# Three-pass output product in the first stage, expert numbers loaded ahead of the waits, and closings by halves in a four-layer kernel

## The chip, the cores and the metric

The kernel runs on 1 core of a Trainium2 chip. The metric is the device time in microseconds, from one launch of the whole program; the time before is the median of 3 runs.

## The reference, cut to what matters

Input x has 32 batches of 64 channels by 1024 columns, 2048 rows in all. Four layers follow each other, each as `x = x + ffn(cond(x))`:

```
L0: cond: 64x64 channel matrix per batch, mixed from 8 by a small softmax net
    ffn:  logits = y route_w^T (8 experts), top 1; h = y A^T (8 x 16 columns);
          out = (gate * h) Bw      -> 2048x128 by 128x1024, the low-rank output product
L1: cond: grouped convolution, 9 taps, plus context; ffn: int8-like quantised 1024x1024 product
L2: cond: grouped convolution; ffn: base 1024x1024 product + bias
          + top 2 of 16 experts: delta = sum_j w_j (y A^T) B_e^T, A^T 1024x64, B_e 64x1024
L3: cond: mixed channel matrix; ffn: relu(y up)^2 down (1024 -> 2048 -> 1024),
          + latent product scaled by the sum of the top 2 gates; then layer norm, gamma, beta
out = x + ...
```

## The kernel before, in words

The rows are cut into 16 tiles of 128 x 1024. Five engines run one instruction list each, written out by hand, and meet through counting semaphores; nothing is planned at run time but loops and the expert numbers. Some TensorE products have f32 operands; most large products are made in three passes of rounded operands (`split_product`, L1992: high by high, high by low, low by high), with the high part a rounded copy and the low part the difference.

**First stage** (`phase_first`, L211). One loop over steps s. In a step TensorE makes: the convolution of tile s-5 in two halves (`conv`, L370) with the channel mixing of tile s between them (L443), a head product (`head`, L345) and transposes of a tile some steps ahead, the output product of tile s-1 (L462: two f32 products of 512 columns, `whT` by `wb`), and the transpose of the gated rows of tile s (L467). ScalarE copies the head (`head_out`, L480), shifts the windows of the convolution of the next step (`shift_windows`, L686, two copies), copies transposed tiles and then `whT` (L540). VectorE adds the context to the convolution's halves (`conv_out`, L575), makes the routing (L629 to L644), the column peaks (L651) and the sum x1 (L662). SP stores x1 (L276), waits until the store has landed, and then loads the convolution's windows of that tile from DRAM in eight transfers (`load_windows`, L679). Ahead of the loop VectorE rounds the weight of layer 1 (`weight_round`, L570), and SP loads weights, among them the taps of both convolutions; the second convolution's taps are read from 242 us on, in the next stage.

**Expert stage** (`phase_l2`, L1276). Pairs of row and expert are sorted into 47 tiles of one expert each (groups of four). For each tile TensorE waits for the part of the operand and for the copies of the tile before last out of its two banks (L1925), loads the expert's number from SBUF into a register (`value_load`, L1926), and makes four passes (L1929). ScalarE and VectorE copy half the result each (L1562, L1769) into one of four buffers, and POOL scatters it to DRAM by an indirect DMA (L1511); a buffer is written again when its DMA has landed. Products of the base weight stand between the groups.

**Last stage** (`phase_l3`, L2000). Tokens are done in two halves of 8 tiles. At the end of each half `downward_both` (L2342) makes a tile's two column halves, 12 passes each, in two banks, and tells VectorE once, behind both. VectorE sums the halves (`add`, L2223), makes the mean (L2282), finishes the tile before (`finish`, L2249: reciprocal of the root, scaling and sum with x, L2256) and centres this one (L2246); ScalarE makes the sum of squares and the root (L2155, L2158); POOL stores each tile (L2123) and waits for the stores at the very end. Behind the first half TensorE's gate product (L2368) waits until all sums are made.

## Time and profile before

| | |
|---|---|
| median of 3 runs | 1641.01 us (1634.74 to 1644.5) |
| profiled execution, own time | 1638.99 us |
| its span | 1637.3 us |
| TensorE products busy | 1571.9 us, 96% |
| VectorE, ScalarE, POOL busy | 822.8, 507.2, 313.1 us |
| mean granted TensorE clock | 0.992 |

The span is the time from the first to the last instruction. Busy times are shares of it; an engine that is not on the chain of waits may be idle at no cost. PE is TensorE's product, PEld its weight load, DVE VectorE, ACT ScalarE, POOL GpSimd, SP SyncE, and a q behind an engine's name (PEq, SPq) its sequencer or queue of DMA issues.

### The profile page before, as it was taken

What the parts mean: (1) busy time and instruction counts of PE and PEld (TensorE: products, weight loads), DVE (VectorE), ACT (ScalarE), POOL (GpSimd) and SP (SyncE); (2) the same over time, 40 slices, a digit from 0 to 9 for tenths busy, and PEclk for the clock granted to TensorE, in tenths of its full rate; (3) what the DMA queues carried; (4) which work ended last, traced back from release to release, by engine and by line L of the source; (5) the groups of instructions that cost most, each with busy time, mean ns of one, the idle gap of its engine ahead of it and who ended that gap; (6) DMA issues with size and microseconds to landing.
All of it is one profiled execution on the core that took longest, in us unless ns stands there. A gap on an engine that the chain in (4) does not pass through costs nothing.

```text
span 1637.3 us, 20655 instructions
## 1 busy us (share of the span) xinstructions
PE 1571.9 (96%) x7752; PEld 1281.6 (78%) x7752; DVE 822.8 (50%) x1336; ACT 507.2 (31%) x763; POOL 313.1 (19%) x262
## 2 busy tenths in 40 slices
PE   8899889999998889999999999999999999999996
PEld 6787668889875568877888888887788888888875
DVE  4767688885574548762333333333633333333336
ACT  4443434433284512223222222212242222222122
POOL 2000022334084520121210011112012100111110
PEclk9999999999999999999999999999999999999998
DMA  9866634556755758883621111115826211111115
GB/s 318 240 191 193 144 118 159 186 191 208 278 174 176 271 180 312 309 306 135 114 81 38 50 51 51 52 52 175 288 77 113 83 38 50 51 51 51 52 41 178
DMA packets 117241, 238.57 MB, mean 146 GB/s; under 512 B 22503, under 2 KB 61551, under 8 KB 115778
## 3 DMA queue, kind: packets, MB, share of 16 engines
q1 hardware_dynamic: 81034, 155.27, 28.8%
q0 software_dynamic: 23008, 68.24, 14.0%
q10 hardware_dynamic: 13120, 14.00, 3.0%
q8 instruction: 51, 0.84, 0.2%
q14 instruction: 28, 0.23, 0.0%
HBM read 164.51 MB, written 89.19 MB: 155 GB/s over the span
## 4 chain that ended last, share of the span: by engine, by line
PE 76%; DVE 5%; POOL 3%; issue 2%; DMA 2%; ACT 1%; SPq 0%; DVEq 0%; POOLq 0%; ACTq 0%
PE pu L1996 27%; PE pd L1996 26%; PE l_po L1996 7%; PE pf L1996 5%; POOL scratch_pairs L1504 2%; PE l_ea L1353 2%; PE pw L675 2%; PE pw L674 2%; PE l_ea L1929 1%; DMA scratch_expert_out<-expert_out,pair_ids 1%; PE l_po L1929 1%; PE l_ea L1944 1%; PE l_tr L1944 1%; DVE y1T L977 0%; PE pd L2368 0%
## 5 line engine op out<-in xcount | busy, mean ns | idle before, releaser
L1996 PE MATMUL pd<-down_hi,hid_hi 128*128 128x512 f32 x640 | 249.1, 389 | 2.9 <-issue 2.9
L1996 PE MATMUL pu<-y_hi,up_hi 128*128 128x512 f32 x640 | 250.7, 392 | 0.6 <-issue 0.6
L1996 PE MATMUL pu<-y_lo,up_hi 128*128 128x512 f32 x640 | 250.3, 391 | 0.0
L1996 PE MATMUL pu<-y_hi,up_lo 128*128 128x512 f32 x640 | 250.2, 391 | 0.0
L1996 PE MATMUL pd<-down_lo,hid_hi 128*128 128x512 f32 x640 | 249.0, 389 | 0.0
L1996 PE MATMUL pd<-down_hi,hid_lo 128*128 128x512 f32 x640 | 249.0, 389 | 0.0
L2297 DVE TENSOR_TENSOR hid_lo<-hidden,hid_hi 128x512 fp32r<-128x512 f32 x64 | 44.3, 693 | 391.5 <-ACT hid_hi L2205 391.5
L2127 POOL TENSOR_TENSOR down_lo<-raw,down_hi 128x1024 fp32r<-128x1024 f32 x40 | 100.5, 2511 | 681.0 <-ACT down_hi L2142 681.0
L2199 ACT ACTIVATE hidden<-pu 128x512 f32<-128x512 f32 x64 | 38.3, 598 | 470.0 <-PE pu L1996 470.0
L2236 DVE TENSOR_TENSOR acc<-pd,acc 128x512 f32<-128x512 f32 x224 | 143.6, 685 | 54.7 <-PE pd L1996 51.4
L1996 PEld LDWEIGHTS pd<-down_hi,hid_hi 128*128 128x128 f32 x640 | 120.1, 188 | 28.7 <-issue 3.7
L1996 PEld LDWEIGHTS pu<-y_hi,up_hi 128*128 128x128 f32 x640 | 121.0, 189 | 26.4 <-issue 1.1
L1996 PEld LDWEIGHTS pu<-y_hi,up_lo 128*128 128x128 f32 x640 | 120.9, 189 | 25.5
L1996 PEld LDWEIGHTS pu<-y_lo,up_hi 128*128 128x128 f32 x640 | 120.8, 189 | 25.0
L1996 PEld LDWEIGHTS pd<-down_lo,hid_hi 128*128 128x128 f32 x640 | 120.3, 188 | 24.9
L1996 PEld LDWEIGHTS pd<-down_hi,hid_lo 128*128 128x128 f32 x640 | 120.1, 188 | 24.8
L1996 PE MATMUL pf<-cbT,z_hi 128*128 128x512 f32 x240 | 97.6, 407 | 5.4 <-DVE z_lo L991 5.4
L1996 PE MATMUL l_po<-l_base_hi,l_y2s_hi 128*128 128x512 f32 x256 | 101.3, 396 | 0.0
L1996 PE MATMUL l_po<-l_base_hi,l_y2s_lo 128*128 128x512 f32 x256 | 99.8, 390 | 0.0
L1996 PE MATMUL l_po<-l_base_lo,l_y2s_hi 128*128 128x512 f32 x256 | 99.8, 390 | 0.0
L1996 PE MATMUL pf<-cbT,z_lo 128*128 128x512 f32 x240 | 94.6, 394 | 0.0
L688 ACT COPY Xs<-X 64x1016 f32<-64x1016 f32 x32 | 33.3, 1040 | 88.4 <-DMA X<-scratch_x 81.6
(329 smaller groups left out, 2495.3 us busy)
## 6 DMA issues: line engine op xcount, KB each, us to landing
l_x<-scratch_x SPq DMA_DIRECT2D x32, 512.0 KB, 6.5
delta<-scratch_expert_out SPq DMA_DIRECT2D x32, 512.0 KB, 7.0
raw<-in_up SPq DMA_DIRECT2D x32, 512.0 KB, 3.7
raw<-in_down SPq DMA_DIRECT2D x32, 512.0 KB, 4.4
X<-scratch_x SPq DMA_DIRECT2D x248, 64.0 KB, 2.6
y1T<-in_x SPq DMA_DIRECT2D x16, 512.0 KB, 8.6
scratch_x<-y1T SPq DMA_DIRECT2D x16, 512.0 KB, 3.3
scratch_x<-l_x SPq DMA_DIRECT2D x16, 512.0 KB, 5.6
```

Source lines behind the costliest of these rows:

```text
L674: pe.matmul(cols, x[:, b * GROUPS + g, :], taps[0][:, g, :], start=True, stop=False)
L675: last = pe.matmul(cols, xs[:, b * GROUPS + g, :], taps[1][:, g, :], start=False, stop=True)
L688: act.copy(xs[0:CH, :, 0:P - 1], x[0:CH, :, 1:P]).then_inc(sem, 1)
L1353: last = pe.matmul(ea[t % 2][:, 0:R2 + E2], prior["y2"][:, t % 2, k, :], war[:, k, :], start=k == 0, stop=k == KC - 1)
L1504: pool.indirect_dma_start(SC["pairs"], bass.IndirectOffsetOnAxis(ap=pos[:, n:n + 1], axis=0), val[:, n, :], None).then_inc(val_stored, 16)
L1929: last = pe.matmul(out_banks[i % 2][h][:], rT[g % 2][part][:, n * P:(n + 1) * P], B[:].rearrange("p e o -> p (e o)")[:, bass.ds(at + h * H ...
L1944: last = pe.matmul(py[t % 2][h][:, c * P:(c + 1) * P], x3[t][:, (4 * h + c) * P:(4 * h + c + 1) * P], mats[:, t % 2, :], start=True, stop= ...
L1996: mm = pe.matmul(out, lhs[a], rhs[b], start=first and n == 0, stop=last and n == len(pairs) - 1)
L2127: pool.tensor_tensor(dn[u][i][1][:], raw[i][:], dn[u][i][0][:].bitcast(F32), ALU.subtract).then_inc(dn_lo, 1)
L2199: act.activation(act_f[:, k % 2, :], pu[q], ACT.Relu).then_inc(relu, 1)
L2236: last = dve.tensor_tensor(part, bank, part, ALU.add)
L2297: dve.tensor_tensor(hid[u][1][:, i, cols], pu[q] if lat else act_f[:, k % 2, :], hid[u][0][:, i, cols].bitcast(F32), ALU.subtract).then_in ...
```

## The change

The low-rank output product of the first stage is made by `split_product` in three passes of rounded parts. The weight is split once ahead of the loop (high by ScalarE, low by VectorE); each step ScalarE rounds `whT` into `whT_hi` behind the copy, and VectorE makes `whT_lo`. The low part of the weight lies where the second convolution's taps lay until now, so these taps are loaded by SP behind the last windows of the stage; the first convolution waits for two taps transfers and no longer for four. The expert number is loaded ahead of the three waits. The closing products signal each column half by itself, VectorE sums them one by one (the last tile of each half: first half, finish of the tile before, second half), and the very last tile is scaled by halves and stored by SP and by ScalarE.

```diff
@@ -204,6 +204,8 @@
     names["h"], names["wh"], names["whT"] = at("h_mixed", 190656, [P, P + E0]), at("wh", 191200, [P, P]), at("whT", 191712, [P, P])
+    names["whT_hi"], names["whT_lo"] = [at("whT_" + part, 192320 + 512 * i, [P, P], F32R) for i, part in enumerate(("hi", "lo"))]
+    names["wb_hi"], names["wb_lo"] = at("l0_wb_hi", 210880, [P, D], F32R), at("l0_wb_lo", 153536, [P, D], F32R)
     names["small"] = at("l0_small", 192224, [P, 24])
...
@@ -286,6 +289,9 @@
                     load_windows(sp, SC["x1"], t, X[t % XS], X_loaded[t % XS], range(0, KC, 1 if t < NT - 2 else 2))
+            sp.wait_ge(o_mm, 2 * NT)
+            for i in range(2):
+                sp.dma_start(K["taps"][1][i][:], A["taps"][1, i]).then_inc(K["taps_loaded"], 16)
 
@@ -370,7 +376,7 @@
                     if t == 0:
-                        pe.wait_ge(K["taps_loaded"], 16 * 4)
+                        pe.wait_ge(K["taps_loaded"], 16 * 2)
                         pe.wait_ge(scb_out, 2)
@@ -452,14 +458,16 @@
                 if 0 <= s - 1 < NT:
-                    pe.wait_ge(whT_made, s)
+                    pe.wait_ge(w_lo, s)
                     if s == 1:
                         pe.wait_ge(agg_out, 8)
+                        pe.wait_ge(wb_split, 2)
                         pe.wait_ge(K["wb_loaded"], 16)
...
                             pe.wait_ge(x1_made, 2 * (s - 2) + i + 1)
-                        pe.matmul(po[i][:], whT[:], wb[:, i * HALF:(i + 1) * HALF], start=True, stop=True).then_inc(o_mm, 1)
+                        cols = slice(i * HALF, (i + 1) * HALF)
+                        split_product(pe, po[i][:], (whT_hi[:], whT_lo[:]), (wb_hi[:, cols], wb_lo[:, cols]), True, True).then_inc(o_mm, 1)
                 if s < NT:
@@ -515,6 +523,8 @@
                     turned_x(t + 2)
+            act.wait_ge(K["wb_loaded"], 16)
+            act.copy(wb_hi[:], wb[:]).then_inc(wb_split, 1)
             for s in range(NT + LAG0 - 1):
@@ -538,6 +548,10 @@
                     act.copy(whT[:], pm[:, 2 * P:3 * P]).then_inc(whT_made, 1)
+                    act.wait_ge(whT_made, s + 1)
+                    if s >= 1:
+                        act.wait_ge(w_lo, s)
+                    act.copy(whT_hi[:], whT[:]).then_inc(w_hi, 1)
                 t = {NT - 1: NT - 2, NT + 1: NT - 1}.get(s)
@@ -617,12 +631,17 @@
                 weight_round(c)
+            dve.wait_ge(wb_split, 1)
+            dve.tensor_tensor(wb_lo[:], wb[:], wb_hi[:].bitcast(F32), ALU.subtract).then_inc(wb_split, 1)
             dve.wait_ge(desc_made, E2)
...
                     conv_out(t, 0)
+                if 1 <= s <= NT:
+                    dve.wait_ge(w_hi, s)
+                    dve.tensor_tensor(whT_lo[:], whT[:], whT_hi[:].bitcast(F32), ALU.subtract).then_inc(w_lo, 1)
                 if s < NT:
@@ -792,6 +811,8 @@
     def conv_half(pe, t, b):
+        if t == 0 and b == 0:
+            pe.wait_ge(K["taps_loaded"], 16 * 4)
         if b == 0:
@@ -1918,12 +1939,12 @@
             g, n = i // 4, i % 4
+            at = pe.value_load(expert_of[0:1, i:i + 1], min_val=0, max_val=(E2 - 1) * D)
             if n == 0:
...
                 pe.wait_ge(eo_dve, i - 1)
-            at = pe.value_load(expert_of[0:1, i:i + 1], min_val=0, max_val=(E2 - 1) * D)
             for h in range(2):
...
@@ -2096,6 +2117,9 @@
                 pair(NPAIR * half + j, j, j % 2, True)
+        sp.wait_ge(last_made, 1)
+        sp.dma_start(tile_of(out, NT - 1)[:, 0:HALF], acc[:, HT - 1, 0:HALF]).then_inc(last_stored, 16)
+        sp.wait_ge(last_stored, 32)
 
@@ -2119,6 +2143,8 @@
                     T = HT * (half - 1) + t
+                    if T == NT - 1:
+                        continue
                     pool.wait_ge(out_made, T + 1)
@@ -2128,7 +2154,7 @@
         steps(body)(pool)
-        pool.wait_ge(out_stored, 16 * NT)
+        pool.wait_ge(out_stored, 16 * (NT - 1))
 
@@ -2212,6 +2238,8 @@
         steps(body)(act)
+        act.wait_ge(last_made, 2)
+        act.dma_start(tile_of(out, NT - 1)[:, HALF:D], acc[:, HT - 1, HALF:D]).then_inc(last_stored, 16)
 
@@ -2220,10 +2248,13 @@
 
-        def add(g, t, half, lat_back, first, end):
-            dve.wait_ge(dn_mm, HT * g + 2 * (t + 1) if end else HT * (g + 1) + t + 1)
+        def add(g, t, half, lat_back, first, end, halves=(0, 1)):
+            if not end:
+                dve.wait_ge(dn_mm, HT * (g + 1) + t + 1)
             T = HT * half + t
-            for h in range(2):
+            for h in halves:
+                if end:
+                    dve.wait_ge(dn_mm, HT * g + 2 * t + h + 1)
                 part, bank = acc[:, t, h * HALF:(h + 1) * HALF], pd[t % 2][h][:]
@@ -2253,8 +2284,14 @@
             dve.wait_ge(x3b_loaded[T % 2], 16 * (T // 2 + 1))
-            dve.scalar_tensor_tensor(out=acc[:, T % HT, :], in0=scratch[:], scalar=inv[:, T:T + 1], in1=x3b[:, T % 2, :],
-                                     op0=ALU.mult, op1=ALU.add).then_inc(out_made, 1)
+            if T < NT - 1:
+                dve.scalar_tensor_tensor(out=acc[:, T % HT, :], in0=scratch[:], scalar=inv[:, T:T + 1], in1=x3b[:, T % 2, :],
+                                         op0=ALU.mult, op1=ALU.add).then_inc(out_made, 1)
+                return
+            for h in range(2):
+                cols = slice(h * HALF, (h + 1) * HALF)
+                dve.scalar_tensor_tensor(out=acc[:, T % HT, cols], in0=scratch[:, cols], scalar=inv[:, T:T + 1],
+                                         in1=x3b[:, T % 2, cols], op0=ALU.mult, op1=ALU.add).then_inc(last_made, 1)
 
@@ -2274,9 +2311,12 @@
                     T = HT * (half - 1) + t
-                    if t == HT - 1:
+                    if t < HT - 1:
+                        add(g, t, half - 1, lat_back, first, end)
+                    else:
+                        add(g, t, half - 1, lat_back, first, end, (0,))
                         finish(T - 1)
-                    add(g, t, half - 1, lat_back, first, end)
+                        add(g, t, half - 1, lat_back, first, end, (1,))
 
@@ -2353,7 +2393,7 @@
                                          [w[:, h * HALF:(h + 1) * HALF] for w in dn[v][i]], n == 0, n == 3)
-            last.then_inc(dn_mm, 2)
+                last.then_inc(dn_mm, 1)
 
@@ -2449,7 +2489,7 @@
         K["kept_loads"] = [(K["l0_wa"][:], A["l0_wa"], K["wa_loaded"]), (K["l0_wb"][:], A["l0_wb"], K["wb_loaded"])]
-        K["kept_loads"] += [(K["taps"][c][i][:], A["taps"][c, i], K["taps_loaded"]) for c in range(2) for i in range(2)]
+        K["kept_loads"] += [(K["taps"][0][i][:], A["taps"][0, i], K["taps_loaded"]) for i in range(2)]
         K["kept_loads"] += [(K["gate"][:], A["gate"], K["l2_loaded"])]
```

Hunks left out only name buffers and semaphores. `split_product` (L1992), which is called now, makes for each pair (high, high), (high, low), (low, high) one matmul into the same bank.

## Rows read from the trace of the kernel before

**Rows 1.** The page; window 507-589 us: busy by engine, clock, DMA share, GB/s.

```profile
span 1637.3 us, 20655 instructions
PE 1571.9 (96%) x7752; PEld 1281.6 (78%) x7752; DVE 822.8 (50%) x1336; ACT 507.2 (31%) x763; POOL 313.1 (19%) x262
...
507.00:589.00 82.00, 63.97 (x255) 42.59 (x256) 41.61 (x72) 39.15 (x70) 43.75 (x45) 0.98 0.65 236
```

**Rows 2.** The page, part 4: the chain that ended last, by engine.

```profile
PE 76%; DVE 5%; POOL 3%; issue 2%; DMA 2%; ACT 1%; SPq 0%; DVEq 0%; POOLq 0%; ACTq 0%
```

**Rows 3.** Timeline of a step of the first stage: start us, us, engine, line, operation [idle before].

```profile
91.86 1.88 PE L462 MATMUL po<-l_wb,whT 128*128 128x512 f32 x4
92.55 1.04 ACT L689 COPY Xs<-X 64x1016 f32<-64x1016 f32 x1
93.58 0.27 PE L467 MATMUL pmix<-ident,wh 128*128 128x128 f32 x1
93.66 0.30 PEld L674 LDWEIGHTS pv<-taps,X 128*128 128x128 f32 x2 [0.36 <-issue]
```

**Rows 4.** The chain in order of time: start us, us, engine, line, passes.

```profile
588.88 10.92 PE l_po L1996 x48
```

**Rows 5.** Timeline of the first stage, steps 14 to 16.

```profile
144.75 0.69 DVE L580 TENSOR_TENSOR y1T<-pv,ctx 128x512 f32<-128x512 f32 x1
146.72 0.29 DVE L644 TENSOR_TENSOR wh<-h_mixed,l_small 128x128 f32<-128x128 f32 x1
150.38 0.69 DVE L580 TENSOR_TENSOR y1T<-pv,ctx 128x512 f32<-128x512 f32 x1
152.74 1.04 ACT L688 COPY Xs<-X 64x1016 f32<-64x1016 f32 x1 [3.88 <-DMA X<-scratch_x]
```

**Rows 6.** Timeline: VectorE at the start, and the two splits of 128x1024.

```profile
46.28 0.35 DVE L629 SCALAR_TENSOR_TENSOR h_mixed<-sumA,bias,pmix 128x136 f32<-128x136 f32 x1
...
1190.86 1.04 ACT L2137 CAST up_hi<-raw 128x1024 fp32r<-128x1024 f32 x1
1191.94 1.23 DVE L2219 TENSOR_TENSOR up_lo<-raw,up_hi 128x1024 fp32r<-128x1024 f32 x1 [0.26 <-ACT up_hi L2137]
```

**Rows 7.** Timeline of SP's queue in the first stage, TensorE behind it; the second convolution's taps (by tile).

```profile
87.84 0.43 SPq L276 DMA_DIRECT2D scratch_x<-y1T  x1
92.33 4.17 SPq L683 DMA_DIRECT2D X<-scratch_x  x8
...
103.34 0.46 PE L674 MATMUL pv<-taps,X 128*128 128x128 f32 x2 [1.05 <-issue]
...
L674 PEld LDWEIGHTS pw<-taps,X x256: 187/192/192, 242.4 to 428.4; 128*128 128x128 f32 x128
```

**Rows 8.** Number load (by line); timeline; waits (us, times, longest).

```profile
L1926 PEldq TENSOR_LOAD <-expert_of x47: 296/548/1207, 506.3 to 586.8; - x47
...
509.58 0.68 DVE L1769 COPY expert_out<-l_ea 128x512 f32<-128x512 f32 x1
511.16 0.49 PE L1929 MATMUL l_ea<-l_B,pair_rT_hi 128*128 x1 [1.81 <-DVE expert_out L1769]
...
PE l_ea L1929 <- DVE expert_out L1769: 10.5, 7, 2.6
```

**Rows 9.** The chain in order of time: a copy, and two landings of the indirect DMA.

```profile
537.17 0.70 DVE expert_out L1769
...
539.24 3.91 DMA scratch_expert_out<-expert_out,pair_ids
...
573.90 8.56 DMA scratch_expert_out<-expert_out,pair_ids
```

**Rows 10.** Timeline and chain of the two closings.

```profile
1176.00 0.40 PE pd L2368
...
1624.65 1.43 DVE acc L2232 x4
...
1629.73 0.53 POOL L2123 DMA_DIRECT2D out<-acc  x1 [4.18 <-DVE acc L2256]
```

More of the change, by code:

```diff
@@ L218, in phase_first @@
             buf[n] for n in ("pack rows agg bk h0 h1 lg ex att m z rz attT ctx12 bias3 scb den quo scb127 tmp xT hp h wh whT small").split()]
+        whT_hi, whT_lo, wb_hi, wb_lo = [buf[n] for n in ("whT_hi", "whT_lo", "wb_hi", "wb_lo")]
         kern, wa, wb, X, Xs = K["kern"], K["l0_wa"], K["l0_wb"], K["X"] + [buf["X"]], K["Xs"] + [buf["Xs"]]
@@ L245, in phase_first @@
         x1_stored, X_loaded = s_.slot_sems("x1_stored", 4), s_.slot_sems("X_loaded", XS)
-        (xT_mm, xT_made, h_mm, hp_made, m_mm, tabled, route, wh_made, wh_turned, whT_made, o_mm, x1_made, Xs_made, conv_done,
+        (xT_mm, xT_made, h_mm, hp_made, m_mm, tabled, wb_split, w_hi, w_lo, route, wh_made, wh_turned, whT_made, o_mm, x1_made, Xs_made, conv_done,
          y_made, topped, early_mm, early_out) = s_.sems(
-            "xT_mm xT_made h_mm hp_made m_mm tabled route_step wh_made wh_turned whT_made o_mm x1_made Xs_made conv_done "
+            "xT_mm xT_made h_mm hp_made m_mm tabled wb_split whT_hi_made whT_lo_made route_step wh_made wh_turned whT_made o_mm x1_made Xs_made conv_done "
             "y1_made y1_topped early_mm early_out")
@@ L2022, in phase_l3 @@
         "gate_mm gateT_made gate_turned gate_out gate_topped gate_summed")
-    gamma_loaded, eps_set, centred, ssq_made, rooted, inverted, weighed, out_made = s_.sems(
-        "gamma_loaded eps_set neg_mean_made sum_sq_made root_made rstd_made weighed out_made")
+    gamma_loaded, eps_set, centred, ssq_made, rooted, inverted, weighed, out_made, last_made, last_stored = s_.sems(
+        "gamma_loaded eps_set neg_mean_made sum_sq_made root_made rstd_made weighed out_made last_made last_stored")
     Q = 2 * NB
```

## The prediction

> **What bounds the kernel now.** I read the page, then the chain that ended last, then the waits and the timeline of the three places that the change touches. The page says that TensorE is busy for 1571.9 of 1637.3 us [rows 1], and the chain runs through its products for most of the span, with only 2% in issue and 3% on POOL [rows 2]. An edit can therefore win only where TensorE itself does less, or where it stands still and the edit touches what it waits for. Three such places are edited: the first stage (0 to 184 us, one tile of 128 rows per step), the expert stage (507 to 589 us, 47 tiles), and the two closings, at 1174 us and at the end. The profiled execution took 1639.0 us round its span of 1637.3; the median of the three runs is 1641.0, 2.0 above it, and the three lie between 1634.7 and 1644.5.
>
> **The product of the first stage.** Each step has one pair of f32 products, 512 columns each. A f32 product shows as two records; the four of a pair begin at 91.86 us, and 1.72 us later, at 93.58, follows the transpose [rows 3]: 0.43 us a record, 0.86 a product. A pass of rounded operands over 512 columns takes 10.92/48 = 0.2275 us [rows 4]. A pair in three passes is 6 x 0.2275 = 1.37 us: TensorE is relieved of 0.36 us a step, 5.7 us in 16 steps. That is the upper end of the gain, and I don't count on it, for what else ends the steps:
>
> In steps 5 to 12 (those with a head product, 8.4 us each) ScalarE copies the head out at 91.19 and then shifts the windows in two copies, the last from 92.55 to 93.59; the weights of the next convolution load at 93.66, after an idle of 0.36 us [rows 3]. TensorE has finished its own queue at the same moment (the transpose begins at 93.58 and holds it for 0.1). A shorter product only lengthens the wait for the shift: gain 0.03 us a step, which I call nothing.
>
> In steps 1 to 3 no windows are waited for and the products stand in line before the next transpose: 3 x 0.36 = 1.1 us gained. In step 4 VectorE ends the wait, so nothing. In steps 13 to 15 VectorE has no gap: its sum of one step begins at 144.75 and that of the next at 150.38, 5.63 us apart and neither behind an idle time [rows 5]. It gets the new subtraction, 128x128; the nearest row is the gated copy of that size at 0.29 us [rows 5]. The windows of the third step on are loaded by SP behind those sums, and ScalarE waits 3.88 us for them at 152.74 [rows 5]; so one such subtraction, +0.3 us, comes on the path, instead of a gain. From 155 us on TensorE runs without a stop to the end of the stage, with one pair in it: -0.36.
>
> The new waits: TensorE's pair waits for the low part, which is made behind VectorE's sum of the convolution (95.75 us) and so at about 96.8, while the next pair begins one period of 8.43 us behind 91.86, at 100.3 [rows 3]: 3 us of cover, under 1 us in steps 13 to 15. ScalarE makes the high part right behind the transposed copy, where nothing waits for it until the next head. On VectorE the routing of the tile is queued behind the subtraction and moves by 0.3 us; its result is wanted over 1 us later. These cost nothing; without cover a step would pay 0.3 + 0.3 us.
>
> The weight's own split is new at the start: a copy of 128x1024 on ScalarE (row of that form: 1.04 us) and a subtraction of 128x1024 on VectorE (1.23 us) [rows 6]. VectorE is the late one there: it rounds weights until 46.28 and starts the first routing at once [rows 6]. The copy fits beside the last rounding, the subtraction doesn't: +1.25 us before the first tile. Less the share of step 1 already won, the first x1 is stored about 0.9 us later. From there SP sets the pace: it stores x1, waits for the landing, then issues eight window loads of 4 us. The store of 87.84 is followed by its windows only at 92.33, when it has landed, and these windows let TensorE begin only at 103.34, after 1.05 us idle [rows 7]. So the 0.9 us arrive there whole, and the 1.1 won on TensorE don't help. The taps of the second convolution leave this queue and go behind the last windows; they are first read at 242.4 us, long after [rows 7]. They stood behind all the weight loads, so nothing comes sooner by it. First stage: +0.9 + 0.3 - 0.36 = +0.85 us. Bounds: -5.7 (every pass saved counts) and +3.7 (1.25 at the start and 0.6 of unhidden copies in four steps).
>
> **Expert numbers.** For each tile TensorE's sequencer waits for the copies of the tile before last, then loads the number (0.30 to 1.21 us, median 0.55), works on registers, and issues [rows 8]. Where the wait was long, the whole comes after it: the copy ends at 510.26 (509.58 + 0.68), and the product starts at 511.16. With the load ahead of the wait about 0.8 of these 0.9 us go. VectorE's copies ended 7 such idle times of 10.5 us in all [rows 8]. A group of four tiles has one long wait; with all 12 groups at 0.8 us the most that can come off is 9.6 us. Where the copies are there in time the load already starts as soon as the previous tile is issued, and the move changes nothing.
>
> What is late next? Each output tile goes: VectorE's copy, POOL's indirect DMA (0.95 + 0.30), its landing, and only then the copy of the tile four later into that buffer. In the trace a copy begins at 537.17, the DMA is issued at 539.24 and has landed at 543.15 [rows 9]: 6.0 us, and 6.3 until the next copy runs. A group of four tiles takes not much more (82 us by 12 is 6.8). So of two groups one is crossed by way of the store, which stays, and one by way of TensorE, where about 1 us goes: 0.5 us a group. Seven groups with such waits give 3.5 us; the first tiles about 0.5, the last ones, behind the long landing of 573.90, about 0.7. I take 0.7 off because the stores come closer together, with the DMA engines already 0.65 busy here [rows 1]. Estimate -4.0 us, between -9.6 and 0.
>
> The Trainium skill, "DMA: Bandwidth & Descriptors", section "Latency and other measured facts", gives a floor of about 600 ns for a tensor load. The trace has loads of 296 ns, so the measurement decides. By the page's figure each hidden load would give 0.6 us and no less, 47 of them 28 us if all stood on the path, which the loop above excludes.
>
> **Closings.** The last tile's two sums take 1.43 us together and begin at 1624.65, because VectorE is finishing the tile before [rows 10]. With a semaphore for each half, the first half of a tile is free 12 passes or 2.7 us sooner, and VectorE sums it in an idle time; that pulls the whole line of VectorE forward by 0.67. On the last tile the order becomes first half, finish of the previous tile, second half: 1622.7, 1623.45, then the second sum from 1624.86 to 1625.53, where it now ends at 1626.08. Gain 0.5. The same in the middle, where the gate's product waits for the sums until 1176.00: another 0.5 [rows 10]. Then the output by halves: POOL's issue runs now from 1629.73 to 1630.26 [rows 10]. Afterwards the second half goes out by ScalarE's queue, as soon as it is scaled; the gap ahead of POOL (0.3 us) and part of its 0.53 go, and the transfer is 256 KB beside 256 KB under way: -0.5. Closings: -1.5 us, bounds -2.5 and -0.5.
>
> The same page's section on one software DMA ("Anatomy of one DMA") gives 2.0 us fixed and the bytes at 436 GB/s: 3.2 us for 512 KB and 2.6 for 256. By that the last landing alone would give 0.6 us, in place of the 0.5 for the whole end of the store. No row here parts a landing into these two.
>
> **Sum.** +0.85 - 4.0 - 1.5 = -4.65 us: 1634.3 for an execution like the profiled one, and about 1636 beside the median of 1641.
>
> **Rivals.** (a) The stores don't bind: their landings stay near 4 us and the expert stage gives its 9.6, the first stage about 0, the closings 1.5. Then -11 us: 1630. For it: most copies in the stage don't wait for a landing. Against: the landing at 573.90 already takes 8.56 us [rows 9]. Chance 0.22. (b) The stores bind wholly, each us saved on TensorE is waited for again at a buffer: expert stage 0, sum -0.65, 1640. For it: landings stand on the chain at 539 and 573 us [rows 9]. Chance 0.20. (c) Slower: in the first stage the delay of the first x1 and the extra VectorE work per step are passed on through SP's chain, 1.25 us at the start and 0.3 us in each of eight or nine steps, +3.7 us, while the expert stage gives under 1 us and the closings 0.5. Sum about +2.5, 1643.5. It decides from the point at which the expert stage gives less than the first stage takes. Chance 0.10. The forecast keeps 0.48.
>
> A measurement of this kernel can't tell under about 0.5% (8 us) from no change. Forecast and (b) lie within it, (c) as well unless the runs scatter; (a) lies beyond. With the scatter of the medians, some 3 us, I give 0.27 to faster, 0.68 to the same, 0.05 to slower. Range: from (a), 1629, to (c), 1643.
>
> **What would show it.** In the trace after: pairs at about 1.37 us with the step still 8.4 us long and a longer idle before the convolution's weights; the first routing at about 47.5; the convolution now at 103.34 at about 104.2; the stage's last VectorE piece near 184.4 instead of 183.6. In the expert stage gaps behind copies of 0.2 to 0.3 us instead of 0.8 and more, and more waits of the copies for landings; the base products behind the stage start near 585.7 after correction for the first stage's shift, instead of 588.9. At the end the last sum ends 0.5 us nearer to the last product. I am wrong if the first stage is shorter by over 1 us (then SP was not its pace), or if the expert stage changes by under 1 or over 7 us.

## The result, and the profile after

The changed kernel takes 1626.80 us, the median of 12 runs (1622.94 to 1634.35), against 1639.34 us for 12 runs of the kernel before: a ratio of 0.9923, interval 0.9906 to 0.994, or 12.5 us faster. In a second series of 6 runs it was 1630.77 against 1639.97, 9.2 us faster. The forecast was 4.65 us and a range down to 1629. The time lay below the range: the direction was right, the size was not.

The profiled execution of the changed kernel happens to be the longest of its 12 (1634.35 us, span 1632.6). Its granted clock is 0.987 on the mean, where before it was 0.992, so whole stages of the two traces are not to be subtracted.

```profile
span 1632.6 us, 20788 instructions
PE 1575.3 (96%) x7784; PEld 1295.0 (79%) x7784; DVE 826.9 (51%) x1354; ACT 511.9 (31%) x780; POOL 310.6 (19%) x261
```

Busy TensorE is 1575.3 us against 1571.9 [rows 1], but at a lower granted clock. The kernel with the three-pass product alone (e1 below), profiled at the clock of the kernel before, 0.992, shows what the passes are worth:

```profile
PE 1567.9 (96%) x7784; PEld 1286.4 (79%) x7784; DVE 824.8 (50%) x1353; ACT 512.5 (31%) x780; POOL 310.9 (19%) x262
```

TensorE is busy for 4.0 us less there, and that kernel is no faster. The time did not come from less work.

**The end.** The first two fences are the transfers by issue (KB each, median us from issue to landing) before and after, the third is the timeline after.

```profile
out<-acc POOLq DMA_DIRECT2D x1, 512.0 KB, 2.9
```

```profile
out<-acc SPq DMA_DIRECT2D x1, 256.0 KB, 2.0
out<-acc ACTq DMA_DIRECT2D x1, 256.0 KB, 2.1
```

```profile
1627.51 1.41 DVE L2293 SCALAR_TENSOR_TENSOR acc<-scratch,l_rstd,l_x3b 128x512 f32<-128x512 f32 x2
1628.29 0.34 SPq L2121 DMA_DIRECT2D out<-acc  x1
1628.96 0.34 ACTq L2242 DMA_DIRECT2D out<-acc  x1
```

Before, the last issue began at 1629.73 [rows 10] and landed 2.9 us later, at 1632.6; the span ended at 1637.3, 4.7 us behind the landing. After, the second half was issued at 1628.96 and landed 2.1 us later, at 1631.1; the span ended at 1632.6, 1.5 us behind it. The timeline has no row for the stretch behind the landing, but the view of the kernel's last source line has: each engine's list is closed by an instruction called DRAIN. Its duration (ns: shortest, median, longest) and start, before and then after:

```profile
L2456 POOLq DRAIN  x1: 3164/3164/3164, 1632.8 to 1632.8; - x1
```

```profile
L2496 POOLq DRAIN  x1: 3082/3082/3082, 1628.2 to 1628.2; - x1
L2496 SPq DRAIN  x1: 7/7/7, 1631.2 to 1631.2; - x1
```

Before, POOL waited for the last landing, began its DRAIN 0.2 us behind it and ended it 3.16 us later, at 1636.0; the remaining 1.3 us are the closing of the program. After, POOL waits for the store before the last, so its DRAIN of 3.08 us runs beside the last store and is over at 1631.3; SP, which waits for the last landing, has a DRAIN of 7 ns at 1631.2. The same 1.3 us follow.

**The expert stage.** Waits (us in total, times, longest) of the copies for a landing, before and after, and the products that wait for a copy after.

```profile
ACT expert_out L1562 <- DMA scratch_expert_out<-expert_out,pair_ids: 10.5, 8, 4.9
DVE expert_out L1769 <- DMA scratch_expert_out<-expert_out,pair_ids: 5.7, 4, 4.3
```

```profile
ACT expert_out L1583 <- DMA scratch_expert_out<-expert_out,pair_ids: 23.6, 23, 3.2
DVE expert_out L1790 <- DMA scratch_expert_out<-expert_out,pair_ids: 14.9, 18, 1.7
PE l_ea L1950 <- DVE expert_out L1790: 6.4, 10, 1.4
```

The copies wait for landings 41 times (38.5 us in all), where it was 12 times (16.2 us). The timeline of a copy and the product behind it:

```profile
529.84 0.69 DVE L1790 COPY expert_out<-l_ea 128x512 f32<-128x512 f32 x1 [0.38 <-DMA scratch_expert_out<-expert_out,pair_ids]
530.82 0.50 PE L1950 MATMUL l_ea<-l_B,pair_rT_hi 128*128 x1 [0.48 <-DVE expert_out L1790]
```

The copy ends at 530.53 and the product starts at 530.82: 0.29 us, in place of 0.90 [rows 8].

**The first stage.** Timeline after, of the start, and of one pair of products in three passes:

```profile
45.95 1.23 DVE L635 TENSOR_TENSOR l_wb_lo<-l_wb,l_wb_hi 128x1024 fp32r<-128x1024 f32 x1
47.09 0.35 DVE L648 SCALAR_TENSOR_TENSOR h_mixed<-sumA,bias,pmix 128x136 f32<-128x136 f32 x1
48.81 0.33 PE L475 MATMUL pmix<-ident,wh 128*128 128x128 f32 x1 [1.20 <-DVE wh L663]
52.85 0.78 PE L2017 MATMUL po<-l_wb_hi,whT_hi 128*128 128x512 f32 x1
54.51 1.52 DVE L681 TENSOR_TENSOR y1T<-po,y1T 128x512 f32<-128x512 f32 x2 [2.36 <-PE po L2017]
...
93.52 0.48 PE L2017 MATMUL po<-l_wb_hi,whT_hi 128*128 128x512 f32 x1
...
95.00 0.27 PE L475 MATMUL pmix<-ident,wh 128*128 128x128 f32 x1
95.43 0.30 PEld L693 LDWEIGHTS pv<-taps,X 128*128 128x128 f32 x2 [0.51 <-issue]
95.46 0.46 PE L693 MATMUL pv<-taps,X 128*128 128x128 f32 x2 [0.18 <-issue]
...
101.98 0.48 PE L2017 MATMUL po<-l_wb_hi,whT_hi 128*128 128x512 f32 x1
```

VectorE's new subtraction puts the first routing at 47.09 instead of 46.28 [rows 6]; TensorE stands still for 1.20 us, and the first three-pass product then shows 0.78 us for a record where a later one shows 0.48: the granted clock had fallen. The windows view (us, busy by engine, granted clock, DMA share, GB/s) of 51 to 55 us and of the stretch behind the middle closing shows it, before and after:

```profile
51.00:55.00 4.00, 3.55 (x20) 2.19 (x18) 2.53 (x5) 1.62 (x4) 0.00 (x0) 1.00 0.07 25
1192.00:1200.00 8.00, 8.00 (x30) 6.42 (x29) 3.35 (x11) 2.57 (x4) 2.46 (x1) 0.79 0.41 131
```

```profile
51.00:55.00 4.00, 3.74 (x14) 3.37 (x15) 1.50 (x6) 1.77 (x4) 0.00 (x0) 0.57 0.00 0
1192.00:1200.00 8.00, 8.00 (x38) 6.71 (x38) 4.13 (x12) 4.21 (x6) 2.48 (x1) 1.00 0.39 126
```

0.57 over 51 to 55 us is nearly all at the lower level, 1.2 GHz. Later, at the full clock, a pair takes 1.48 us, from 93.52 to 95.00, where it was 1.72 [rows 3]. The idle time ahead of the next convolution's weights is longer instead, as foreseen: 0.51 us where it was 0.36 [rows 3]; and the next pair begins at 101.98, 8.46 us behind this one, where the step was 8.43 us long. A shorter product, the same step.

### The profile page after: what moved, and what is told of

Read it like the earlier page. It is cut to its first block, busy times and chain, and to the rows that moved or that the text cites. A ratio compares the mean times of both kernels' runs of the same rounds, so it can differ in the third digit from the quotient of the medians.

```text
span 1632.6 us, 20788 instructions
## 1 busy us (share of the span) xinstructions
PE 1575.3 (96%) x7784; PEld 1295.0 (79%) x7784; DVE 826.9 (51%) x1354; ACT 511.9 (31%) x780; POOL 310.6 (19%) x261
## 4 chain that ended last, share of the span: by engine, by line
PE 76%; DVE 5%; DMA 3%; POOL 2%; issue 2%; ACT 1%; SPq 0%; DVEq 0%; POOLq 0%; ACTq 0%
PE pu L2017 27%; PE pd L2017 26%; PE l_po L2017 7%; PE pf L2017 6%; POOL scratch_pairs L1525 2%; DMA scratch_expert_out<-expert_out,pair_ids 2%; PE l_ea L1374 2%; PE pw L694 2%; PE pw L693 2%; PE l_ea L1965 1%; PE l_tr L1965 1%; PE pg L1142 1%; DVE expert_out L1790 0%; DVE y1T L998 0%; PE pd L2408 0%
## 5 line engine op out<-in xcount | busy, mean ns | idle before, releaser
L2017 PEld LDWEIGHTS pf<-cbT,z_hi 128*128 128x128 f32 x240 | 47.5, 198 | 18.6 <-DVE z_lo L1012 8.8
```

Source lines behind the costliest of these rows:

```text
L2017: mm = pe.matmul(out, lhs[a], rhs[b], start=first and n == 0, stop=last and n == len(pairs) - 1)
```

## Marks that can be compared

In every profile I read the same places: the start of the first sum x1; the start of the last column maximum of the first stage; the first and last start of an expert product; the start of the last product; the end. A dip is a stretch at the lower level of the granted clock. Most dips cost TensorE 1.7 us each (their width times 1 - granted clock), the longer ones a multiple of that; "at full clock" takes the sum of these costs off a stretch. The kernels are grouped by what they contain, so a row rests on many executions, not on one.

```
mark                        without the part               with the part
first x1                    52.7 (9 profiles)              54.6 (5: product as changed)
last maximum of stage 1     183.4 (182.2 to 185.2)         183.5 (182.2 to 185.5)
expert products, 1st-last   79.7 (9; 77.7 to 82.0)         76.6 (9; 72.5 to 82.2: load ahead)
  the same at full clock    77.5 (76.0 to 79.4)            72.6 (70.8 to 73.8)
last stage, to last product 893.3 (6)                      891.1 (12: sums by halves)
  of it 1st half, no dip    452.3                          451.7
last product to the end     13.4 (3 profiles)              8.7 (10; 8.6 to 8.8)
```

By these marks the whole change is worth -4.7 us at the end, -2.2 in the last stage ahead of it, -3.1 in the expert stage and +0.1 in the first: -9.9 us, between the 9.2 and the 12.5 of the two series.

## Experiments

Three parts alone, and the whole again on the same chip. "e1" has only the hunks of the first stage, "e2" only this one, "e3" only those of the last stage:

```diff
+            at = pe.value_load(expert_of[0:1, i:i + 1], min_val=0, max_val=(E2 - 1) * D)
             if n == 0:
                 pe.wait_ge(r_lo, g + 1)
...
-            at = pe.value_load(expert_of[0:1, i:i + 1], min_val=0, max_val=(E2 - 1) * D)
```

> The kernel before with the three-pass product, its splits and the moved taps, and nothing else of the change. Theory A (the steps of the first stage end on ScalarE's window shift, on VectorE and on SP's queue, so the passes saved on TensorE are not worth time): between -1 and +1.5 us against before, about +0.5; the last VectorE piece of the stage near 184.4 us where no clock dip falls in it. Theory B (the passes count, 16 steps of 0.36 us): -5 to -6 us, and the large gain of the whole change comes for half from here.

Measured: 1641.65 us, ratio 1.0002 (0.9983 to 1.002). First x1 at 54.5, last maximum at 182.9. B falls, for its -5 us would be a ratio of 0.997. A stands (+0.3 us by the ratio, +1.7 by the medians): the passes are not worth time.

> The kernel before with the expert number loaded ahead of the three waits, and nothing else. Theory A (the load's latency comes off wherever TensorE waits for a copy, and the scatter's landing binds afterwards): -5 to -7 us, the first expert product to the last one 75 us apart where it was 81, and the copies waiting for landings over 30 times where it was 12. Theory B (what was forecast, two groups of which one is crossed by way of the store): -4 us. Theory C (stores bind wholly): 0 to -1 us.

Measured: 1638.31, ratio 0.9993 (0.9976 to 1.0009); 79.3 us from first to last expert product, 72.5 at full clock, with 22 waits for landings. The time alone speaks for C, the full-clock mark for A, and the 3.1 us of all profiles in the table lie nearest to B. The stretch had 6.8 us of dips in this profile, the kernels without the part 2.2 on the mean.

> The kernel before with the closing sums by halves and the last tile by halves on SP and ScalarE, and nothing else. Theory A (the end of the output store was under-priced: from the end of the last scaling to the end of the span 7.9 us before and 3.7 after): about -5 us, of it -4 behind the last scaling, -0.5 to -0.7 in the last sums and -0.5 in the middle. Theory B (the forecast): -1.5 us. If the mid closing also spares a dip of TensorE's clock (0.79 granted at 1192 to 1200 us before, 1.00 after), another -1.7 us.

Measured: 1631.83, ratio 0.9947 (0.9927 to 0.9967): -8.1 us. 8.7 us from the last product to the end. The largest part of the gain is here, more even than theory A said.

> The changed kernel once more, on the chip of the three single parts. Theory A: about -12 us, and the three parts add up to it within 2 us. Rival: the parts add up to clearly less or more, so that one part spends or covers what another wins (for instance fewer dips of the clock only where both stand together). Its profile tells how far the dips of the clock in the first 350 us (0.91 in 45 to 65 and in 105 to 125 us) belong to the kernel: if they come back at the same places they do, if not they are scatter of single executions.

Measured: 1630.77, ratio 0.9949 (0.9929 to 0.9969). The parts add up to -8.1 (+1.7 - 1.7 - 8.1) beside the -9.2 of this series, as A says, and fall short of the -12.5 of the first. The mean granted clock was 0.9897 in these runs of the changed kernel and 0.9914 in those; with the slope given at the end of the text that alone is an estimated 2.3 us of the 4.0 between the two medians. The dip at 50 us is in this profile and in e1's as well, the one at 105 is in neither. In SP's queue the late start can be followed; first the window loads before, then in e4:

```profile
122.62 3.62 SPq L683 DMA_DIRECT2D X<-scratch_x  x8
137.44 4.72 SPq L683 DMA_DIRECT2D X<-scratch_x  x8
```

```profile
124.52 3.62 SPq L702 DMA_DIRECT2D X<-scratch_x  x8
137.43 4.91 SPq L702 DMA_DIRECT2D X<-scratch_x  x8
```

The load is 1.9 us late at 124.52 and on time at 137.43. So SP hands the delay on for 70 us, as said, but the loop behind takes it back.

**What of the end gives the time.** e5 stores the last tile whole by SP, e6 by halves by POOL, e7 has only the sums by halves:

```diff
# e5
+        sp.wait_ge(last_made, 1)
+        sp.dma_start(tile_of(out, NT - 1), acc[:, HT - 1, :]).then_inc(last_stored, 16)
+        sp.wait_ge(last_stored, 16)
# e6
+        for h in range(2):
+            pool.wait_ge(last_made, h + 1)
+            pool.dma_start(tile_of(out, NT - 1)[:, h * HALF:(h + 1) * HALF], acc[:, HT - 1, h * HALF:(h + 1) * HALF]).then_inc(out_stored, 16)
```

> The kernel before; only the very last output tile is stored whole by SP's queue, behind one whole scaling, and SP waits for it, in place of POOL's. Sums and everything else as before. From the last product to the end of the span it is 13.4 us before and 8.7 with all the closings. Theory A (the queue of POOL is what costs: its landing of 4.2 us and 2 to 3 us between that landing and the end): about 10.5 us, so 3 us of the 4.7. Theory B (the halving is what gives, smaller transfers and half a scaling): over 12.5 us.

Measured: 9.7 us from the last product to the end; 1637.39, ratio 0.9988 (0.9971 to 1.0004). Timeline, then its transfer:

```profile
1631.61 1.28 DVE L2265 SCALAR_TENSOR_TENSOR acc<-scratch,l_rstd,l_x3b 128x1024 f32<-128x1024 f32 x1
1632.92 0.34 SPq L2100 DMA_DIRECT2D out<-acc  x1
```

```profile
out<-acc SPq DMA_DIRECT2D x1, 512.0 KB, 2.6
```

Landed at 1635.5, span 1637.0: 1.5 us. A holds: the last store on another engine gives 3.7 of the 4.7 us. POOL's DRAIN is as long as ever, but it runs from 1632.2 to 1635.3, beside the store that SP waits for:

```profile
L2465 POOLq DRAIN  x1: 3082/3082/3082, 1632.2 to 1632.2; - x1
```

The Trainium skill, "DMA: Bandwidth & Descriptors", section "Specifications", puts the first byte at about 1 us by POOL's path and 0.6 by SP's or ScalarE's. As an estimate from these figures of the page, SP's queue in place of POOL's is worth 0.4 us. The trace agrees on that part, 2.6 us from issue to landing in place of 2.9. Of the 3.7 us, 3.2 lie behind the landing and 0.3 ahead of the issue.

> The kernel before; the very last tile is scaled and stored by halves, but both stores stay with POOL. Theory A (the queue): 12.8 to 13.5 us from the last product to the end, under 0.6 us gained. Theory B (the halving): 10.5 us or less. What was forecast for the store (-0.5 us) would be met here.

Measured: 13.3 us; 1639.00, ratio 0.9993 (0.9978 to 1.0009). The halves save 0.2: POOL issues them one behind the other,

```profile
1632.76 1.21 POOL L2135 DMA_DIRECT2D out<-acc  x2 [3.65 <-DVE acc L2267]
```

the second at 1633.42, it lands at 1635.9 (2.5 us), and the span ends at 1640.6, again 4.7 later, with a DRAIN of 3.25 us in it. B falls.

> The kernel before; only the semaphores and sums of the closing products by column halves, middle and end, with the finish of the tile before between the last two sums; the store is as before. Forecast for it: 0.5 us at the end (12.9 from the last product to the end of the span instead of 13.4) and 0.5 in the middle. After the traces with all the closings: 0.65 at the end, 0.7 in the middle.

Measured: 12.8 us from the last product to the end, and 451.8 from the last stage's first product to that behind the middle closing, where the kernel before has 454.0 with a dip and 452.3 at full clock; 1637.17, ratio 0.999 (0.9977 to 1.0004). At the end 0.7, as expected. In the middle 0.6 at full clock, and dips beside it: between 1175 and 1200 us dips stand in 3 of the 6 profiles with the old sums (5 dips), in none of the 12 with the new ones. (e11 and e12 below keep the old sums too, and both have one at this place.) That the sums by halves keep the clock up is what these counts suggest; no run tries it by itself.

**Is it the store by POOL, or POOL's waiting?** e10: POOL stores as before, SP waits.

```diff
-        pool.wait_ge(out_stored, 16 * NT)
+        sp.wait_ge(out_stored, 16 * NT)   # at the end of SP's program
```

> The kernel before; POOL issues all output stores as before, but the last wait for their landing is made by SP, and POOL ends with its last issue. In the kernel before 4.7 us pass from the last landing to the end of the span, with the last tile on SP 1.5. Theory A (POOL itself is slow to see the landing or to close): 10.0 to 10.5 us from the last product to the end, as with the store on SP, -3.2 us. Theory B (the software queue is late with its signal, whoever waits): 13.2 to 13.5, no gain.

Measured: 11.7 us, between the two; 1635.89, ratio 0.9972 (0.9956 to 0.9987).

```profile
1631.39 0.53 POOL L2124 DMA_DIRECT2D out<-acc  x1 [4.18 <-DVE acc L2256]
```

With 2.9 us to land, as in the kernel before, the end at 1637.2 is 2.9 us behind the landing at 1634.3: 1.8 of the 3.2 go with POOL's waiting, 1.4 stay. The view of the last source line says where they go:

```profile
L2456 POOLq DRAIN  x1: 4510/4510/4510, 1631.4 to 1631.4; - x1
L2456 SPq DRAIN  x1: 7/7/7, 1634.4 to 1634.4; - x1
```

POOL's DRAIN begins with its issue, for POOL waits no longer, and ends at 1635.9; SP is through at 1634.4. The end waits for POOL once more. Nobody is slow to see a landing (in the kernel before POOL goes on within 0.1 us of it), and the landing is no later than before, so neither theory has the cause: it is the DRAIN that closes POOL's list, about 3.1 us behind a last wait and 4.0 us behind the end of a last issue. It is hidden only where POOL's last work with a DMA lies far enough ahead of the last landing. What the instruction does in that time no run shows.

**The late start.** e8 makes the low part of the weight by POOL; e9 keeps the first product in f32 and makes the low part in VectorE's gap; e13 (and e18, the same again) keeps the first five in f32 and makes it behind the sum of step 5:

```diff
# e8, on POOL ahead of its wait for h_mm
+            pool.tensor_tensor(wb_lo[:], wb[:], wb_hi[:].bitcast(F32), ALU.subtract).then_inc(wb_split, 1)
# e13, on VectorE behind the sum x1 of step 5 (e9: ahead of that of step 1)
+                if s == 5:
+                    dve.tensor_tensor(wb_lo[:], wb[:], wb_hi[:].bitcast(F32), ALU.subtract).then_inc(wb_split, 1)
# e13, TensorE (e9: s == 1)
+                        if s <= 5:
+                            pe.matmul(po[i][:], whT[:], wb[:, cols], start=True, stop=True).then_inc(o_mm, 1)
+                            continue
```

> The changed kernel, with the low part of the low-rank weight made by POOL, idle there, and no longer by VectorE. Theory A (VectorE's 1.23 us put off the first tiles, TensorE stood 1.2 us and its clock fell to half for 3.4 us in 50 to 55 us in all three kernels with the product, in none without): first sum x1 at 52 to 52.5 us instead of 54.5, no dip at 50, stage end 2 us sooner, so about 1.5 to 2 us less than the changed kernel. Theory B (SP's chain of landings sets the pace from the first tile on, or a dip comes a bit later instead): under 0.5 us. Theory C: POOL takes the shared port or its 2.5 us from VectorE's roundings, and the first routing moves by over 1 us anyway.

Measured: 1626.94, ratio 0.9934 (0.9913 to 0.9955); first x1 at 55.4, later than without the edit. Theory C:

```profile
46.39 2.36 POOL L325 TENSOR_TENSOR l_wb_lo<-l_wb,l_wb_hi 128x1024 fp32r<-128x1024 f32 x1 [5.53 <-ACT l_wb_hi L529]
46.80 1.97 DVE L654 SCALAR_TENSOR_TENSOR l_small<-h_mixed,l_small,desc 128x8 f32<-128x8 f32 x1
```

A routing instruction on 128x8, 0.23 us in the changed kernel, lasts 1.97 while POOL subtracts; TensorE stands for 1.67 us, and the dip comes all the same. VectorE's instruction ends at 48.77, POOL's at 48.75.

The Trainium skill, "SBUF — State Buffer", section "SBUF: two separate sides", says that a VectorE operation with two inputs in SBUF and a POOL operation that reads SBUF lock each other out for a whole instruction. The trace agrees: these two end 0.02 us apart, while VectorE's instruction with one input just ahead, at 46.60 and beside POOL too, took its usual 0.16.

> The changed kernel; the very first output product (step 1) stays in f32, and VectorE makes the low part of the weight in its gap of 1.27 us ahead of the first sum x1 instead of ahead of the first routing (the low part lies in another place, and a load of the latent stage goes behind the last product for it). Theory A (VectorE's 1.23 us ahead of the first routing make TensorE stand and then fall to half its clock at 50 to 55 us): first x1 at 52.4 to 52.8 us instead of 54.5, no dip at 50, the last VectorE piece of the stage near 180.5 to 181 us, and 1.5 to 2 us under the changed kernel. Theory B (SP's landings take it back, or the dip only moves): under 0.5 us.

Measured: 1636.08, ratio 0.9974 (0.9959 to 0.9989), 9.3 and 5.3 us over the two medians of the changed kernel. The start was as A said (x1 at 52.3, no dip), but TensorE waited 9.5 us at 156 for the load of `latent_exp` that I had put behind the last product; the latent product needs it there. The run says nothing on the rest.

> The changed kernel; the output products of the first five steps stay in f32, and VectorE makes the low part of the weight behind the sum x1 of step 5, where the steps are 8.4 us long and it has 2 us and more to spare; nothing else is moved. Theory A (the 1.23 us ahead of the first routing cost the start): first x1 at 52.4 us instead of 54.5, no dip of the clock at 50, the last VectorE piece near 180 us instead of 182.2 and more, and 2 to 3 us under the changed kernel, about 1625. Theory B (later waits take it back): under 1 us.

Measured: 1626.96, ratio 0.9914 (0.9892 to 0.9936). x1 at 53.0, no dip at 50; yet the last maximum is at 186.8, with one idle time of 3.4 us before a convolution behind a window load.

> The kernel with the first five output products in f32 once more, with the all-but-product kernel on the same chip. Theory A: the stage ends at 180 to 182 us where no window load lands late, and the median is 1.5 us and more under that of all but the product. Theory B (SP's loads set the end of the stage, whatever TensorE and VectorE save): the two are within 1.5 us of each other, and the windows of steps 12 to 15 end the waits again.

Measured: 1631.91, ratio 0.9956 (0.9935 to 0.9976); x1 at 52.5, last maximum at 182.8. Theory B: the early start reaches the first x1 and not the end of the stage. The two medians of one and the same kernel, on two chips and each beside its own runs of the kernel before, are 13.8 and 7.7 us below those. This is the size of what a median of 6 to 12 runs does not settle here.

**Leaving one part out.** e14 is the change without the number load ahead, e15 with the last tile stored by POOL (sums by halves stay), e17 without anything of the product; e16 is e3 again.

> The changed kernel with the number load behind the waits, as before. Theory A (the load ahead gives 4 to 4.5 us in the expert stage): 79 to 80 us between the first and the last expert product, and 4 us over the changed kernel, -6 against before. Theory B (the median of the load alone, -1.7 us, is the true size): under 2 us over the changed kernel.

Measured: 1632.53, ratio 0.9948 (0.9928 to 0.9967); 78.2 us, 76.5 at full clock. That is 5.7 and 1.8 us over the two medians of the changed kernel, or 4.3 and 1.0 with each set against its own runs of the kernel before. The times don't part A from B; the mark at full clock, 3.9 us over the 72.6 of the table, speaks for A.

> The changed kernel with the last tile scaled whole and stored by POOL, as before; the sums stay by halves. Theory A (the queue of the last store is worth 4.1 us in any company): 12.8 us from the last product to the end, 4.1 over the changed kernel, -6 to -7 against before. Theory B (the store is worth more than its marks, as the median of the closings alone suggests): 6 us or more over the changed kernel.

Measured: 1632.76, ratio 0.9952 (0.9931 to 0.9973); 12.8 us at the end, so 4.1 us for the store, as A says. The medians are 6.0 and 2.0 over the changed kernel (4.5 and 1.2 against the kernel before), so the times leave B open.

> The kernel before with the closings alone, once more. If the -8.1 us of the first time were scatter of TensorE's clock between executions, it comes now nearer to what its marks give, -5.4 us (-4 to -7); if they belong to the kernel, -8 again, with a mean granted clock above that of before by 0.003 again.

Measured: 1631.81, ratio 0.9951 (0.9933 to 0.9969): 8.95 us under the kernel before. The mean granted clock of its runs is 0.9914, that of all runs of the kernel before 0.9893. The larger gain of the closings is no accident of one chip. The marks give 4.7 at the end and 0.6 in the middle, the dips at the middle some 1.5; the last 1 to 2 us I can't place.

> The changed kernel without anything of the product: first stage and taps as before, number load ahead and closings as changed. Theory A (what the passes give in the loop, 2.2 us, the late start with its dip of the clock takes back): within 1.5 us of the changed kernel, about -11 us against before. Theory B (the product gives something beside the other parts that it doesn't give alone): 3 us or more over the changed kernel.

Measured: 1633.01, ratio 0.997 (0.995 to 0.9991); last maximum at 182.2. It is 6.6 us under its kernel before, where A said 11, and 6.2 and 2.2 us over the two medians of the changed kernel, on both sides of B's 3 us. By the times the question stays open. For A speak that it is 1.1 us over e18 on the same chip, inside the scatter, and that nothing in the first stage of the two profiles shows a gain by the product; its expert stage was the one with most dips (8.5 us).

**Fewer scatters.** e11 and e12 leave out the store of every second expert tile, whose buffer is free at once; e12 has the load ahead too.

```diff
+            if i % 2:
+                pool.sem_inc(eo_stored[i % 4], 16)
+                continue
```

> The kernel before; every second output tile of the experts is not stored, its buffer is free at once (and the table of outputs is filled with finite numbers by one long transfer in the first stage, which makes that stage longer; only the expert stage is read). It takes half the load off the scatter. Theory A (in the kernel before, TensorE's own load behind its wait is the larger part, landings the smaller): the expert products take 77 to 79 us from first to last, where five kernels with this stage unchanged took 77.7 to 82.0. Theory B (landings bind already before): 73 us or less.

> As the run with half the scatters, and the expert number loaded ahead of the waits. Theory A (with the load ahead the landings bind: 41 waits of the copies for them, where it was 12): 69 to 71 us, clearly under the 72.5 to 79.3 of the kernels with all scatters, and under the run with half the scatters alone by 7 us or more. Theory B (landings hardly count even then; TensorE and its copies set the pace): 73 to 75 us.

Measured, one profile each: 77.4 and 72.6 us from first to last expert product; at full clock 72.3 and 70.0. So without the load ahead, half the scatters give 2.3 us (5.2 at full clock), and with it 4.0 (2.6). Neither wait is the whole: A for e11 by its raw number; e12 lies between A and B, and 4.8 us under e11 where A said 7 or more. The load ahead is worth 4.9 us at full clock with all scatters and 2.3 with half of them. The two savings overlap. Each number rests on a single profile, and profiles that share one and the same expert stage lie up to 3 us apart at full clock.

## Why the prediction was wrong

**The step that failed is the end of the store.** The forecast gave -0.5 us to "the gap ahead of POOL (0.3 us) and part of its 0.53", and -1.5 to all closings. Measured: 4.1 us for the store, 0.7 for the last sums (0.5 forecast), 0.6 in the middle (0.5 forecast) and about 1.5 more there by dips of the clock that stopped. I priced the issue and the bytes and took no account of what lies behind the landing, though it stood in rows I had: issue at 1629.73 [rows 10], end of the span at 1637.3 [rows 1], 7.6 us, of which the landing is 2.9. A chain of waits ends with the last issue and does not show the rest. The rest is the DRAIN that closes POOL's list, 3.16 us and begun only when POOL's wait for the last landing was over; e5 takes the last store from POOL and the time behind the landing falls from 4.7 to 1.5 us, e6 halves the store and leaves it with POOL and nothing falls, e10 shows that the store alone, without POOL's wait, still keeps 1.4 of it. Of the 4.1 us about 3 lie there; about 1 lies where the forecast looked, in the gap ahead of the issue (0.3 us) and the landing (2.9 us, now 2.1), twice what it took. With this one term at 4.1 the sum would have been -8.3.

**Expert stage, -4.0 forecast.** Measured -3.1 raw, -4.9 at full clock; leaving it out of the change cost 2 to 6 us by the medians, 1 to 4 against the kernels before. The picture of the forecast held: gaps of 0.3 us, landings that end the waits in place of TensorE (41 times), and a gain well under the 9.6 of rival (a). Rival (b) falls too, by the marks; the time of e2 alone would not exclude it. Not foreseen: the stage has more dips of the clock with the load ahead (4.0 us in place of 2.2 on the mean), which gives back 1.8 us. Why was not tried.

**First stage, +0.85 forecast.** Measured +0.1 at its end, between marks that scatter by 3 us. The start is later than I said: x1 by 1.9 and not 0.9. The dip at 50 us is in all six profiles with the weight's split ahead of the loop, and in 4 of 14 others; of these, e10, e16 and e17 have the old product and x1 at 53.4 to 53.8, so between profiles with the dip the split costs 1.1 us, near the forecast, and the rest is the dip. The loop gave back 1.8, of which I had counted only the 0.36 at its end. A pair takes 1.48 us and not the 1.37 of the sum, so the passes free 0.24 us a step and not 0.36: 3.8 us and not 5.7 in 16 steps, as busy TensorE shows (4.0 less in e1). The main claim, that they don't become time, stands: e1 shows no gain.

**Rivals and range.** The measured time is nearest to rival (a), 1630, and for another reason than (a) gave: who had bet on (a) would have been near by luck. Rival (c) didn't come: the start's delay was not passed on to the end. The range ended at 1629 with rival (a), whose closings were the forecast's own; no bound of it looked at the time behind the last landing. The forecast also held that a measurement can't tell under 8 us from no change; the 12 runs gave an interval of 2.8 us to either side.

A correction to the description of the change: it is the high part of the weight that lies where the second convolution's taps were; the low part overwrites the weight itself. (That is why e13 can subtract only behind its last f32 product.) No number hangs on it.

## What to carry to other kernels

Subtract the last issue from the end of the span before pricing a last store, and look at what closes each engine's list: POOL's took 3.1 us here and started only behind POOL's last wait. The store by other engines was worth eight times the gain forecast. In the changed kernel POOL's DRAIN ends at 1631.3 and SP's at 1631.2, so the two are level now, and a still shorter last store would give next to nothing while POOL waits for the one before it (an estimate from these two ends). A saving of TensorE's passes is worth time only where TensorE ends the step; a subtraction put in front of its first dependency can cost more than its duration, where the clock falls behind the idle time. Where kernels differ by 2 to 4 us and one kernel's executions scatter by 10, marks inside many profiles tell more than medians.

## What the runs showed of the hardware

- The DRAIN that closes POOL's list took 3.08 to 3.25 us behind POOL's last wait for a DMA, and 4.51 where it began with the issue; SP's took 7 ns. So a store issued and waited for by POOL ended the program 4.7 us behind its landing, one of SP or ScalarE 1.5 to 1.7, and one issued by POOL with SP waiting 2.9.
- While POOL subtracted 128x1024 (2.36 us), a VectorE instruction on 128x8 took 1.97 us and not 0.23. It shows as busy time, not as a wait.
- Most dips of TensorE's granted clock cost 1.7 us of its time each. The mean clock of an execution goes with its length: within the kernels (272 runs, those of the kernel before among them) 0.001 less comes with 1.36 us more, with a correlation of 0.79, so much of the scatter goes with such dips.
